# Two more value units on GpSimd, and a new order of the first two rows, in a graph-attention kernel

## The chip, the cores and the metric

The kernel runs on one core of one Trainium2 chip. The metric is the device time of one execution in microseconds (us), the median of a few executions. TensorE is called PE below, VectorE DVE, ScalarE ACT, GpSimd POOL and SyncE SP, as in the profile.

## What is computed

The reference normalises x (8192 x 256), takes the ReLU of it, averages the result over the neighbours in a dense 8192 x 8192 integer adjacency matrix with attention weights, and adds x. The attention's two score vectors f1 and f2 come from a second input through one small linear layer.

```python
h = jnp.maximum(_layernorm(x, axis=-1), 0.0)
# inside the layer: inlayer = h
hid = inlayer2 @ W.T + b
f1, f2 = hid @ w1 + b1, hid @ w2 + b2
logits = f1[:, None] + f2[None, :]
coefs = softmax(leaky_relu(logits, 0.01) + where(adj > 0, 0, -1e9), axis=-1)
return x + coefs @ inlayer
```

## The kernel before, in words

**Steady state.** The output's 8192 rows are taken 128 at a time, as 64 row tiles `I`. For one row tile the 8192 neighbours are two chunks `c` of 4096, and the weights of a chunk are made in four parts `g` (a group of 32 rows each) and turned in four strips, so that a row tile has eight parts and eight strips `k` of 1024 neighbours. The steps for one row tile are:

- SP loads the adjacency of a chunk into `adj_sb` (512 KB per transfer, four of them a chunk, one for each quadrant of partitions; `load_adj`, L335).
- ACT turns a part into a mask (`mask_part`, L540, recorded at L554). From row tile 1 on the mask lies in `mask` in SBUF; for row tile 0 it lies in PSUM rooms that are free then (`rp`, `acc`; `row0_mask`, L132).
- DVE makes the weights of a part (`weights`, L817, recorded at L824) from the packed words `b_word` and `c_word` and the mask, and turns each strip (`turn`, L828, recorded at L834) into one of four slots of `wT`.
- PE multiplies a strip with the values `H` (`products`, L1013): 8 blocks of 128 neighbours, three matmuls of 257 columns for each, two at L1024 (high and low part of the value, times the high part of the weight) and one at L1026. That is 24 matmuls a strip.
- DVE, ACT and POOL finish the row tile (`finish_0` to `finish_2`, `scale_rows`, `finish`), and SP stores it.

**Before the steady state** two things are made that all row tiles need. The first is the score part: the second input is loaded, turned on DVE (L718) and multiplied on PE (L979), and from f2 come the exponentials `D_big`, `D_inv` and b on ACT (L615, L616, L537), c (L622), and the packed words on DVE (`pack`, L807, recorded at L809 and L810). The second is the values: x is loaded in eight strips of 1024 rows (`load_x`, 256 KB a transfer, the quadrants 0 and 1 from SP's queue and 2 and 3 from ACT's queue, L333). The row statistics come from ACT for strips 0 and 1 (`sums`, `squares`, L584) and from DVE for the others (`raw_stats`, L765, and `variance`, L773). POOL makes 1/sqrt of the variance (`rstds`, a power, L411) and from it a factor and an offset for each row (`affine`, L423 to L433).

A **value unit** `n` is 512 rows (four blocks of 128 rows), 16 in all, two for each strip. `values(n)` applies the factor and the offset: four instructions of 256 columns, on ACT with a ReLU (L570) or, for the units in `values_on_pool`, on POOL without it (L460). `high_of_values(n)` writes the 16-bit high part, always on ACT (L576), with a ReLU. `low_of_values(n)` writes the low part: even units on POOL (L467), odd ones on DVE (L804), which takes the maximum with 0 first. Unit n uses float32 room n % 4, so it waits until the high and low part of unit n - 4 are there (`wait_slot`, L312). `D_column(k)` on POOL (L451) adds the column that gives the denominators. `sum_of_values(k)` on PE (L1038) sums the values of a strip with 16 + 16 small matmuls.

**Order.** Each engine works through its own list in the written order, and waits on semaphores of the others. For row tiles 0 and 1 the lists are written out by hand and interleaved with the making of the values: POOL's at L482 to L519, ACT's at L600 to L675, DVE's at L776 to L797 and L856 to L920, PE's at L1042 to L1072. PE's order is strips 0 to 3 of row tile 0 (with the sums of values 0 to 3), strips 0, 1, 2 of row tile 1, strip 4 of row tile 0, strip 3 of row tile 1, strip 5 of row tile 0, the sums 4 and 5, strips 4 and 5 of row tile 1, strip 6 of row tile 0, sum 6, strip 7 of row tile 0, strip 6 of row tile 1, sum 7, strip 7 of row tile 1. Then it waits for `h_sum` (DVE, L918) and makes the mean of the values (L1071), and row tile 2 begins. Strip 0 of row tile 0 (`products(0, 0, 0)`) needs turn (0, 0), the high and low parts of units 0 and 1, and `D_column(0)`; a later strip k of row tile 0 needs the same of units 2k and 2k + 1. Strips of row tile 1 need only their turn.

`two_rows` (L277) is the order in which the masks and the weights of row tiles 0 and 1 are made; the semaphore counts come from it. `first_adj` and `second_adj` (L354, L358) are the places where ACT's queue issues its half of the adjacency of row tiles 0 and 1; SP issues the other half.

Of the kernel before, what the change touches and what calls it, by code (L numbers as in the profile page):

```python
# [45 lines left out]
def graph_attention(nc, x, adj, inlayer2, W, b, w1, b1, w2, b2, out):  # L46
# [26 lines left out]
    with ExitStack() as ctx:  # L73
# [200 lines left out]
        def is_row(I, n):  # L274
            return type(I) is int and I == n

        two_rows = ((0, 0, 0), (0, 1, 0), (0, 2, 0), (0, 3, 0), (0, 0, 1), (0, 1, 1), (1, 0, 0),  # L277
                    (1, 1, 0), (1, 2, 0), (1, 3, 0), (0, 2, 1), (0, 3, 1), (1, 0, 1), (1, 1, 1),
# [23 lines left out]
        values_on_pool = (3, 7, 11, 15)  # L302
# [90 lines left out]
        def _(pool):  # L393
# [89 lines left out]
            rstds(2)  # L483
            scale_D()
            affine(0)
            rstds(1)
            rstds(3)
            affine(1)
            parts_of_D()
            low_of_values(0)  # L490
            values(3)
            affine(2)
            D_column(0)
            affine(3)
            low_of_values(2)
            rstds(4)
            D_column(1)
            low_of_values(4)
            values(7)
            D_column(2)  # L500
            D_column(3)
            affine(4)
            low_of_values(6)
# [6 lines left out]
            D_column(4)  # L510
            low_of_values(10)
            rstds(7)
            D_column(5)
            affine(7)
            values(15)
            D_column(6)
            low_of_values(12)
            D_column(7)
            low_of_values(14)  # L519
# [4 lines left out]
        def _(act):  # L524
# [94 lines left out]
            b_of_chunk(1)  # L619
            values(0)  # L620
# [22 lines left out]
            high_of_values(6)  # L643
            high_of_values(7)
            mask_part(0, 1, 1)
# [4 lines left out]
            mask_part(0, 2, 1)  # L650
# [41 lines left out]
        def _(dve):  # L692
# [88 lines left out]
            raw_stats(20, 24)  # L781
# [4 lines left out]
            variance(2)  # L786
            raw_stats(24, 28)
# [73 lines left out]
            weights(0, 0, 0)  # L861
            raw_stats(36, 40)
            raw_stats(40, 44)
            weights(0, 1, 0)
            weights(0, 2, 0)
            variance(4)
            raw_stats(44, 48)
            weights(0, 3, 0)
            raw_stats(48, 52)
            turn(0, 0)  # L870
            low_of_values(1)
            low_of_values(3)
            turn(0, 1)
            raw_stats(56, 60)
            raw_stats(52, 56)
            variance(5)
            turn(0, 2)
            variance(6)
            turn(0, 3)
            low_of_values(5)  # L880
            low_of_values(7)
            weights(0, 0, 1)
            weights(0, 1, 1)
# [5 lines left out]
            weights(0, 2, 1)  # L889
# [3 lines left out]
            raw_stats(60, 64)  # L893
            low_of_values(9)
            turn(0, 4)
            variance(7)
            turn(1, 3)
            low_of_values(11)
            weights(1, 0, 1)
            turn(0, 5)  # L900
# [10 lines left out]
            weights(2, 0, 0)  # L911
            weights(2, 1, 0)
# [5 lines left out]
            nc.vector.tensor_scalar(h_sum[:, :], hs_ps, 1.0 / (H_SCALE * N), None, ALU.mult).then_inc(h_sum_ready, 1)  # L918
            weights(2, 2, 0)
# [41 lines left out]
        def _(pe):  # L961
# [142 lines left out]
```

## Time and profile before

| | |
|---|---|
| median of 3 runs | 1448.58 us (1448.45 to 1448.86) |
| the profiled execution's own time | 1447.21 us |
| its span | 1445.4 us |
| PE busy | 1408.1 us (97%) |
| DVE busy | 1279.7 us (89%) |
| ACT busy | 612.4 us (42%) |
| POOL busy | 267.6 us (19%) |
| chain that ended last: PE acc L1024 and L1026 | 61% and 30% of the span |
| HBM | 209 GB/s over the span |

The span is the time from the first to the last instruction of the program. The profile takes PE as busy while a matmul is in flight, and matmuls overlap: the mean L1024 matmul is recorded at 273 ns, but one starts every 110 ns. A group's "idle before" is the time in which the engine did nothing just before its instructions, with the releaser that ended most of it.

### The profile page before, as it was taken

What the parts mean: (1) busy time and instruction counts of PE and PEld (TensorE: products, weight loads), DVE (VectorE), ACT (ScalarE), POOL (GpSimd) and SP (SyncE); (2) the same over time, 40 slices, a digit from 0 to 9 for tenths busy, and PEclk for the clock granted to TensorE, in tenths of its full rate; (3) what the DMA queues carried; (4) which work ended last, traced back from release to release, by engine and by line L of the source; (5) the groups of instructions that cost most, each with busy time, mean ns of one, the idle gap of its engine ahead of it and who ended that gap; (6) DMA issues with size and microseconds to landing.
All of it is one profiled execution on the core that took longest, in us unless ns stands there. A gap on an engine that the chain in (4) does not pass through costs nothing.

```text
span 1445.4 us, 33386 instructions
## 1 busy us (share of the span) xinstructions
PE 1408.1 (97%) x12623; PEld 1246.3 (86%) x12623; DVE 1279.7 (89%) x1313; ACT 612.4 (42%) x714; POOL 267.6 (19%) x269
## 2 busy tenths in 40 slices
PE   8489999999999999999999999999999999999998
PEld 7377888888888888888888888888888888888887
DVE  5899999989899898989989898998989989898994
ACT  2895344344444343444434344343434434344430
POOL 0582111101111110111111011111101111110111
PEclk9789999999999999999999999999999999999999
DMA  9978999999999999999999999999999999999940
GB/s 301 310 181 181 234 230 230 231 232 220 208 211 215 209 211 209 215 209 210 215 209 210 207 216 211 209 215 209 210 207 217 209 211 215 207 212 207 215 103 8
DMA packets 110168, 302.43 MB, mean 209 GB/s; under 512 B 11716, under 2 KB 44612, under 8 KB 110148
## 3 DMA queue, kind: packets, MB, share of 16 engines
q1 hardware_dynamic: 100144, 289.58, 89.4%
q10 hardware_dynamic: 10004, 12.59, 2.9%
q8 instruction: 12, 0.20, 0.1%
q14 instruction: 8, 0.07, 0.0%
HBM read 293.73 MB, written 8.39 MB: 209 GB/s over the span
## 4 chain that ended last, share of the span: by engine, by line
PE 94%; ACT 2%; DVE 2%; DMA 1%; issue 1%; ACTq 0%; POOL 0%; SPq 0%; POOLq 0%; DVEq 0%
PE acc L1024 61%; PE acc L1026 30%; PE rp L979 2%; DMA adj_sb<-in_adj_dram 1%; DVE wgt L824 1%; ACT h_f L570 1%; DVE wT L834 0%; ACT H L576 0%; PE rp L993 0%; ACT o_room L584 0%; DMA w<-in_L_gnn_w_dram 0%; PE small L966 0%; ACT rp L554 0%; DVE b_word L810 0%; ACT mask L554 0%
## 5 line engine op out<-in xcount | busy, mean ns | idle before, releaser
L1024 PE MATMUL acc<-H,wT 128*128 128x257 f16 x8192 | 1356.2, 273 | 9.7 <-DVE wT L834 6.9
L1026 PE MATMUL acc<-H,wT 128*128 128x257 f16 x4096 | 1120.0, 273 | 0.0
L1024 PEld LDWEIGHTS acc<-H,wT 128*128 128x128 bf16 x8192 | 802.1, 98 | 113.0 <-DVE wT L834 6.9
L554 ACT ACTIVATE mask<-adj_sb 128x1024 bf16<-128x1024 int32 x504 | 519.2, 1053 | 542.8 <-DVE wgt L824 428.8
L834 DVE STREAM_TRANSPOSE wT<-wgt 128x1024 f32<-128x1024 f32 x512 | 634.0, 1239 | 129.2 <-PE acc L1026 129.1
L824 DVE SCALAR_TENSOR_TENSOR wgt<-b_word,c_word,mask 128x1024 f32<-128x1024 f32 x504 | 626.9, 1256 | 0.0
L1026 PEld LDWEIGHTS acc<-H,wT 128*128 128x128 f16 x4096 | 401.5, 98 | 50.5
L474 POOL TENSOR_TENSOR x_res<-o_room,x_res 128x256 f32<-128x256 f32 x64 | 66.5, 1039 | 1115.2 <-ACT o_room L561 1069.5
L561 ACT ACTIVATE o_room<-acc,r_den 128x256 f32<-128x256 f32 x64 | 30.2, 471 | 251.0 <-DVE r_den L853 251.0
L479 POOL TENSOR_TENSOR o_room<-o_room,x_res 128x256 f32<-128x256 f32 x64 | 82.3, 1287 | 5.3
L476 POOL TENSOR_SCALAR o_room<-h_mean,no_nb 128x256 f32<-128x256 f32 x64 | 60.8, 950 | 0.0
L979 PE MATMUL rp<-wT,h_f 128*128 128x256 f32 x128 | 28.0, 381 | 0.0
L979 PEld LDWEIGHTS rp<-wT,h_f 128*128 128x128 f32 x128 | 24.5, 192 | 3.3
L570 ACT ACTIVATE h_f<-H,h_add,h_mul 128x256 f32<-128x256 f32 x48 | 24.7, 588 | 1.0 <-issue 1.0
L467 POOL TENSOR_TENSOR H<-h_f,H 128x1024 f16<-128x1024 f32 x8 | 17.8, 2226 | 4.0 <-ACT H L576 4.0
L411 POOL TENSOR_TENSOR rstd<-var_eps,minus_half 128x8 f32<-128x8 f32 x8 | 14.7, 1845 | 13.8 <-DVE var_eps L773 13.7
L1045 PE MATMUL small<-ones 128*128 128x128 f32 x20 | 4.6, 429 | 11.8 <-DVE wgt L824 11.8
L765 DVE BATCH_NORM_STATS2 stats<-H 128x6 f32<-128x512 f32 x24 | 15.3, 688 | 0.8 <-DMA H<-in_x_dram 0.8
L843 DVE TENSOR_SCALAR no_nb<-acc 128x1 f32<-128x1 f32 x64 | 7.7, 120 | 9.2 <-PE acc L1026 9.2
L1045 PEld LDWEIGHTS small<-ones 128*128 128x128 f32 x20 | 4.3, 331 | 12.0 <-DVE wgt L824 12.0
L718 DVE STREAM_TRANSPOSE wT<-wgt 128x1024 f32<-128x1024 f32 x8 | 9.5, 1222 | 5.7 <-DMA wgt<-in_L_gnn_inlayer_dram 3.6
L718 DVE STREAM_TRANSPOSE wT<-adj_sb 128x1024 f32<-128x1024 f32 x8 | 9.5, 1225 | 4.3 <-PE rp L979 4.3
(91 smaller groups left out, 173.2 us busy)
## 6 DMA issues: line engine op xcount, KB each, us to landing
adj_sb<-in_adj_dram SPq DMA_DIRECT2D x504, 512.0 KB, 8.6
x_res<-in_x_dram SPq DMA_DIRECT2D x64, 128.0 KB, 4.0
out_dram<-o_room SPq DMA_DIRECT2D x64, 128.0 KB, 4.2
H<-in_x_dram ACTq DMA_DIRECT2D x16, 256.0 KB, 12.2
H<-in_x_dram SPq DMA_DIRECT2D x16, 256.0 KB, 12.7
adj_sb<-in_adj_dram ACTq DMA_DIRECT2D x8, 512.0 KB, 13.1
wgt<-in_L_gnn_inlayer_dram ACTq DMA_DIRECT2D x8, 256.0 KB, 9.0
wgt<-in_L_gnn_inlayer_dram SPq DMA_DIRECT2D x8, 256.0 KB, 9.6
```

What stands on the lines that cost most here:

```text
L474: nc.gpsimd.tensor_tensor(x_res[:, par, :], o_raw[:, par, :], x_res[:, par, :], ALU.add).then_inc(pool_step, 1)
L476: nc.gpsimd.tensor_scalar(o_sb[:, par, :], h_mean[:, :], no_nb[:, par:par + 1], None, ALU.mult).then_inc(pool_step, 1)
L479: nc.gpsimd.tensor_tensor(o_sb[:, par, :], o_sb[:, par, :], x_res[:, par, :], ALU.add).then_inc(o_ready, 1)
L554: nc.scalar.activation(place, adj_sb[:, c, g * CQ:(g + 1) * CQ], ACT.Relu, scale=M_SCALE).then_inc(m_ready, 1)
L561: nc.scalar.activation(o_raw[:, par, :], acc[:, par, 0:D], ACT.Copy, scale=r_den[:, par:par + 1]).then_inc(scaled, 1)
L570: nc.scalar.activation(h_slot(n)[:, t, :], x_stage(n // 2)[:, j % TS, :], ACT.Relu, scale=h_mul[:, j:j + 1], bias=h_add[:, j:j + 1]).then_ ...
L718: nc.vector.transpose(in2T[:, k % 2, :, :].rearrange("p m (t s) -> p t m s", t=TS)[:, HALF * e:HALF * (e + 1), :, :], in2_stage(k)[:, HALF ...
L824: nc.vector.scalar_tensor_tensor(out=wgt[:, wgt_slot(I, c), g, :], in0=b_word[:, c * CQ:(c + 1) * CQ], scalar=c_word[:, bass.ds(Q * I + g, ...
L834: nc.vector.transpose(wT[:, wT_slot(I, k), :, :].rearrange("p t (g r) -> p g t r", g=Q), wgt[:, wgt_slot(I, c), :, s * SQ:(s + 1) * SQ]).t ...
L979: mm = pe.matmul(rp[:, k // SC, SQ * (k % SC):SQ * (k % SC + 1)], V[:, m, :], in2T[:, k % 2, m, :], start=(m == 0), stop=(m == FM - 1))
L1024: pe.matmul(acc[:, par, 0:DV], w_hi[:, slot, t, :], H[:, j, part, 0:DV], start=(j == 0 and part == 0), stop=False)
L1026: mm = pe.matmul(acc[:, par, 0:DV], w_lo[:, slot, t, :], H[:, j, 0, 0:DV], start=False, stop=(j == ROWS - 1))
```

## The change

`values_on_pool` gets the units 5 and 13 beside 3, 7, 11 and 15, so POOL makes the affine part of six units and ACT of ten. On ACT's list x strips 4 and 5 are issued after `squares(1)`, strip 6 after the exponentials of b, strip 7 after `high_of_values(0)`, and `f_to_sbuf(0)` comes after `squares(0)`. In `two_rows` part (0, 2, 1) comes before row tile 1's first parts. POOL, ACT and DVE get new orders for the first two row tiles: on DVE `low_of_values(1)` comes before turn (0, 0), two pairs of statistics come after it, part (0, 2, 1) comes before row tile 1's, and parts (2, 0, 0) and (2, 1, 0) come after `h_sum`. On PE `sum_of_values(4)` comes one place earlier. Nothing is changed from row tile 2's strips on, and no computation is added or left out.

```diff
-        two_rows = ((0, 0, 0), ..., (0, 0, 1), (0, 1, 1), (1, 0, 0),
-                    (1, 1, 0), (1, 2, 0), (1, 3, 0), (0, 2, 1), (0, 3, 1), ...
+        two_rows = ((0, 0, 0), ..., (0, 0, 1), (0, 1, 1), (0, 2, 1),
+                    (1, 0, 0), (1, 1, 0), (1, 2, 0), (1, 3, 0), (0, 3, 1), ...
-        values_on_pool = (3, 7, 11, 15)
+        values_on_pool = (3, 5, 7, 11, 13, 15)
-            rstd_order = (0, 2, 1, 3, 4, 5, 6, 7)
+            rstd_order = (0, 1, 3, 2, 4, 5, 6, 7)
```

POOL's list after the change, in full:

```python
rstds(0); rstds(1); scale_D(); affine(0); parts_of_D(); rstds(3); rstds(2); affine(1); affine(2)
values(3); D_column(0); D_column(1); low_of_values(0); affine(3); values(5); low_of_values(2)
D_column(2); low_of_values(4); values(7); low_of_values(6); rstds(4); D_column(3); affine(4)
rstds(5); rstds(6); affine(5); affine(6); values(11); low_of_values(8); D_column(4); values(13)
D_column(5); low_of_values(10); rstds(7); affine(7); low_of_values(12); D_column(6); values(15)
low_of_values(14); D_column(7)
```

ACT's list (the core of the diff):

```diff
             sums(0)
             load_x(act, 1, 2, (2, 3))
-            f_to_sbuf(0)
             load_x(act, 2, 3, (2, 3))
             squares(0)
             load_x(act, 3, 4, (2, 3))
+            f_to_sbuf(0)
             first_adj(act, 0, (2, 3))
-            load_x(act, 4, 5, (2, 3))
             sums(1)
             f_to_sbuf(1)
+            squares(1)
+            load_x(act, 4, 5, (2, 3))
             load_x(act, 5, 6, (2, 3))
-            squares(1)
-            load_x(act, 6, 7, (2, 3))
-            load_x(act, 7, 8, (2, 3))
...
             b_of_chunk(0)
             b_of_chunk(1)
+            load_x(act, 6, 7, (2, 3))
+            mask_part(0, 0, 0)
             values(0)
...
+            values(1)
             high_of_values(0)
-            mask_part(0, 0, 0)
+            load_x(act, 7, 8, (2, 3))
             mask_part(0, 1, 0)
             first_adj(act, 1, (2, 3))
             mask_part(0, 2, 0)
-            mask_part(0, 3, 0)
-            values(1)
             high_of_values(1)
             values(2)
+            mask_part(0, 3, 0)
             high_of_values(2)
+            values(4)
             second_adj(act, 0, (2, 3))
-            values(4)
             high_of_values(3)
             high_of_values(4)
-            values(5)
             high_of_values(5)
```

DVE's list from the packed words to the end of the two row tiles (w is `weights`, t `turn`, lo `low_of_values`, st `raw_stats` by its first block):

```text
before: pack; st32; w(0,0,0); st36; st40; w(0,1,0); w(0,2,0); var4; st44; w(0,3,0); st48; t(0,0); lo1; lo3; t(0,1);
        st56; st52; var5; t(0,2); var6; t(0,3); lo5; lo7; w(0,0,1); w(0,1,1); w(1,0..3,0); t(1,0); w(0,2,1);
        t(1,1); w(0,3,1); t(1,2); st60; lo9; t(0,4); var7; t(1,3); lo11; w(1,0,1); t(0,5); w(1,1..3,1); t(1,4);
        t(1,5); t(0,6); lo13; t(0,7); t(1,6); lo15; w(2,0,0); w(2,1,0); t(1,7); finish 0; h_sum; w(2,2,0); w(2,3,0)
after:  pack; st32; w(0,0,0); st40; st36; st44; w(0,1,0); lo1; w(0,2,0); w(0,3,0); var4; t(0,0); var5; t(0,1);
        lo3; t(0,2); st48; t(0,3); st52; w(0,0,1); w(0,1,1); var6; lo5; lo7; w(0,2,1); w(1,0..3,0); t(1,0); st56;
        t(1,1); w(0,3,1); t(1,2); lo9; t(0,4); st60; t(1,3); var7; t(0,5); lo11; w(1,0..3,1); t(1,4);
        t(1,5); t(0,6); lo13; t(0,7); t(1,6); lo15; t(1,7); finish 0; h_sum; w(2,0,0); w(2,1,0); w(2,2,0); w(2,3,0)
```

## Rows read from the trace of the kernel before

**Rows 1.** The page's part 5: PE's costliest group and the waits before it.

```profile
L1024 PE MATMUL acc<-H,wT 128*128 128x257 f16 x8192 | 1356.2, 273 | 9.7 <-DVE wT L834 6.9
```

**Rows 2.** Busy time by stretch: length, then PE, PEld, DVE, ACT, POOL, PEclk, DMA share, GB/s.

```profile
90.60:93.50 2.90, 2.86 (x14) 2.02 (x15) 2.90 (x3) 2.90 (x7) 2.90 (x4) 0.51 1.02 275
...
140.00:1440.00 1300.00, 1299.55 (x11815) 1155.69 (x11812) 1161.54 (x1164) 523.41 (x546) 202.86 (x186) 1.00 0.93 206
```

**Rows 3.** Timeline of PE: start us, length us, engine, line, operation, count [idle before, releaser].

```profile
70.95 0.59 PE L1024 MATMUL acc<-H,wT 128*128 128x257 f16 x2 [2.74 <-DVE H L804]
...
90.64 0.61 PE L1024 MATMUL acc<-H,wT 128*128 128x257 f16 x2 [4.28 <-DVE wT L834]
...
110.06 0.40 PE L1024 MATMUL acc<-H,wT 128*128 128x257 f16 x2 [0.57 <-DVE wT L834]
...
124.25 0.61 PE L1038 MATMUL small<-H,D_inv_parts 128*2 128x256 f16 x16
...
129.15 0.38 PE L1024 MATMUL acc<-H,wT 128*128 128x257 f16 x2 [1.11 <-DVE wT L834]
...
132.58 0.39 PE L1024 MATMUL acc<-H,wT 128*128 128x257 f16 x2 [0.63 <-DVE wT L834]
```

**Rows 4.** Timeline of ACT and its queue (ACTq), 46 to 58 us.

```profile
46.46 2.85 ACTq L333 DMA_DIRECT2D H<-in_x_dram  x1
...
49.34 1.42 ACTq L333 DMA_DIRECT2D H<-in_x_dram  x1
50.80 0.26 ACT L615 ACTIVATE D_big<-f_rel 128x64 f32<-128x64 f32 x1 [3.27 <-issue]
...
51.11 2.10 ACT L537 ACTIVATE wgt<-rp,tiny 128x1024 f32<-128x1024 f32 x2
53.10 2.08 ACT L570 ACTIVATE h_f<-H,h_add,h_mul 128x256 f32<-128x256 f32 x4
...
55.34 1.06 ACT L576 ACTIVATE H<-h_f 128x1024 f16<-128x1024 f32 x1
...
56.28 1.97 ACT L554 ACTIVATE rp<-adj_sb 128x1024 f32<-128x1024 int32 x2
```

**Rows 5.** Timeline of DVE, from f2_rel to row tile 2.

```profile
48.48 0.25 DVE L790 TENSOR_SCALAR f_rel<-f_col,tiny 128x64 f32<-128x64 f32 x1
...
50.50 0.17 DVE L773 TENSOR_SCALAR var_eps<-stats 128x8 f32<-128x8 f32 x1
52.24 0.76 DVE L809 TENSOR_SCALAR b_word<-wgt 128x1024 bf16<-128x1024 bf16 x1 [1.58 <-ACT wgt L537]
...
57.42 1.30 DVE L765 BATCH_NORM_STATS2 stats<-H 128x6 f32<-128x512 f32 x2
...
77.88 1.18 DVE L804 SCALAR_TENSOR_TENSOR H<-h_f,H 128x1024 f16<-128x1024 f32 x1
79.09 3.05 DVE L804 SCALAR_TENSOR_TENSOR H<-o_room,H 128x1024 f16<-128x1024 f32 x1
...
96.33 2.87 DVE L804 SCALAR_TENSOR_TENSOR H<-h_f,H 128x1024 f16<-128x1024 f32 x1
...
124.91 0.42 DVE L918 TENSOR_SCALAR h_sum<-small 128x256 f32<-128x256 f32 x1 [2.30 <-PE small L1038]
125.25 2.47 DVE L824 SCALAR_TENSOR_TENSOR wgt<-b_word,c_word,mask 128x1024 f32<-128x1024 f32 x2
```

**Rows 6.** Timeline of POOL, 60 to 115 us.

```profile
61.89 2.17 POOL L460 TENSOR_SCALAR o_room<-H,h_mul,h_add 128x256 f32<-128x256 f32 x4
...
78.18 2.88 POOL L467 TENSOR_TENSOR H<-h_f,H 128x1024 f16<-128x1024 f32 x1 [0.37 <-ACT H L576]
81.02 4.23 POOL L411 TENSOR_TENSOR rstd<-var_eps,minus_half 128x8 f32<-128x8 f32 x2
...
104.46 5.22 POOL L460 TENSOR_SCALAR o_room<-H,h_mul,h_add 128x256 f32<-128x256 f32 x4
...
112.02 2.13 POOL L467 TENSOR_TENSOR H<-h_f,H 128x1024 f16<-128x1024 f32 x1
```

More of the change, by code:

```diff
@@ L482, in _ @@
             rstds(0)
-            rstds(2)
+            rstds(1)
             scale_D()
             affine(0)
-            rstds(1)
+            parts_of_D()
             rstds(3)
+            rstds(2)
             affine(1)
-            parts_of_D()
+            affine(2)
+            values(3)
+            D_column(0)
+            D_column(1)
             low_of_values(0)
-            values(3)
-            affine(2)
-            D_column(0)
             affine(3)
+            values(5)
             low_of_values(2)
-            rstds(4)
-            D_column(1)
+            D_column(2)
             low_of_values(4)
             values(7)
-            D_column(2)
+            low_of_values(6)
+            rstds(4)
             D_column(3)
             affine(4)
-            low_of_values(6)
             rstds(5)
@@ L510, in _ @@
             D_column(4)
+            values(13)
+            D_column(5)
             low_of_values(10)
             rstds(7)
-            D_column(5)
             affine(7)
+            low_of_values(12)
+            D_column(6)
             values(15)
-            D_column(6)
-            low_of_values(12)
+            low_of_values(14)
             D_column(7)
-            low_of_values(14)
             pool.wait_ge(h_mean_done, 1)
@@ L643, in _ @@
             high_of_values(6)
+            mask_part(0, 1, 1)
+            mask_part(0, 2, 1)
             high_of_values(7)
-            mask_part(0, 1, 1)
             mask_part(1, 0, 0)
@@ L780, in _ @@
             chunk_f(1)
-            raw_stats(20, 24)
+            raw_stats(24, 28)
             dve.wait_ge(u_ready, Q + 1)
@@ L785, in _ @@
             nc.vector.reduce_max(tiny[0:1, 1:2], fm_ps, AX.X).then_inc(f_max_ready, 1)
-            variance(2)
-            raw_stats(24, 28)
+            raw_stats(20, 24)
             dve.wait_ge(F_ps_ready, 1)
@@ L792, in _ @@
             nc.vector.tensor_scalar(tiny[:, 3:4], F_ps, SLOPE - 1.0, None, ALU.mult).then_inc(f_offset_ready, 1)
+            variance(2)
             raw_stats(28, 32)
+            variance(3)
             then_wait(nc.vector.tensor_tensor(tiny[:, 5:6], tiny[:, 4:5], tiny[:, 2:3], ALU.add))
@@ L861, in _ @@
             weights(0, 0, 0)
+            raw_stats(40, 44)
             raw_stats(36, 40)
-            raw_stats(40, 44)
+            raw_stats(44, 48)
             weights(0, 1, 0)
+            low_of_values(1)
             weights(0, 2, 0)
+            weights(0, 3, 0)
             variance(4)
-            raw_stats(44, 48)
-            weights(0, 3, 0)
-            raw_stats(48, 52)
[L870 to L874, printed above, removed]
+            turn(0, 0)
+            variance(5)
+            turn(0, 1)
+            low_of_values(3)
+            turn(0, 2)
+            raw_stats(48, 52)
+            turn(0, 3)
             raw_stats(52, 56)
-            variance(5)
-            turn(0, 2)
+            weights(0, 0, 1)
+            weights(0, 1, 1)
             variance(6)
-            turn(0, 3)
             low_of_values(5)
             low_of_values(7)
-            weights(0, 0, 1)
-            weights(0, 1, 1)
+            weights(0, 2, 1)
             weights(1, 0, 0)
@@ L888, in _ @@
             turn(1, 0)
-            weights(0, 2, 1)
+            raw_stats(56, 60)
             turn(1, 1)
@@ L892, in _ @@
             turn(1, 2)
-            raw_stats(60, 64)
             low_of_values(9)
             turn(0, 4)
+            raw_stats(60, 64)
+            turn(1, 3)
             variance(7)
-            turn(1, 3)
+            turn(0, 5)
             low_of_values(11)
             weights(1, 0, 1)
-            turn(0, 5)
             weights(1, 1, 1)
@@ L918, in _ @@
             nc.vector.tensor_scalar(h_sum[:, :], hs_ps, 1.0 / (H_SCALE * N), None, ALU.mult).then_inc(h_sum_ready, 1)
+            weights(2, 0, 0)
+            weights(2, 1, 0)
             weights(2, 2, 0)
```

25 lines of the change are left out of this document (10 added, 15 removed).

## The prediction

> **What bounds the kernel now.** I read the page's groups first, then the busy time by stretch, then the timelines of the first 140 us. PE is the bound of nearly everything: from 140 to 1440 us it starts 11,815 matmuls in 1300 us, one every 0.110 us, at full clock and without idle time [rows 2]. All PE's waits for turned strips are 6.9 us [rows 1], and they lie before 133 us. From the last wait of 0.63 us at 132.58 [rows 3] on, the rest of the kernel is fixed: it ends 1445.4 - 132.6 = 1312.8 us later. The change leaves it alone, so its worth is how far that point (strip 1 of row tile 2, "the anchor") moves. A shift of 2.9 us is 0.2% of the time, which is about what a measurement of this kernel can tell from no change.
>
> Before the anchor PE waits at 70.95 (2.74 us), 90.64 (4.28), 110.06 (0.57), 129.15 (1.11) and 132.58 (0.63), each time but the first for a turn, and the first for a low part, all from DVE [rows 3]. DVE, in turn, has one idle time of note before it packs b: 1.58 us, waiting for ACT's exponential [rows 5]. From 52.24 to the turn that the strip at 110.06 waited for it works without a gap. So up to strip 4 of row tile 1 (PE at 110.06) **DVE is the bound**; from there to 124.25 + 0.6 = 124.85, the end of the last sum of values, PE is, with 14.8 us of its own work; then DVE again: `h_sum`, two weights, a turn, two weights, a turn, 7.7 us up to the anchor.
>
> **The change, part by part.** I sum along DVE's list.
>
> *The x issues behind the exponentials.* ACT's queue issued strip 7's two transfers for 2.85 and 1.42 us, and D_big waited 3.27 us for nothing else ("issue"); it began at 50.80 [rows 4]. In the new order strips 4 and 5 are issued there, not 6 and 7, so the queue holds four transfers fewer than when strip 7's had to wait, and I expect short issues. DVE has f2_rel at 48.48 + 0.25 [rows 5], so D_big starts at 48.9; the two small exponentials and the first b (0.3 + 1.05 us) are done at 50.3. DVE is free only at 50.50 + 0.17 [rows 5], with the same small steps to do in the new order. It packs at 50.75 instead of 52.24: **1.5 us gained**. Bounds: 0 if the issues block as before, 1.6 if DVE is free a little sooner. The transfers issued later are covered: ACT's queue still has its adjacency transfers in flight at 46 us, keeps its order, and strip 4's data are wanted by DVE only after the packing, at 56 us. SP's list and its issues are unchanged. In the worst case DVE's statistics wait as long as the issue is late, a microsecond or two, and that is in the range.
>
> *DVE's work up to turn (1, 4).* Both lists hold the same instructions between the packing and this turn (16 of L765, 16 weights, 6 low parts, the turns), so reordering them costs nothing by itself. What differs is what they run into. A low part on DVE takes 1.18 us (at 77.88) [rows 5]. The one at 79.09 took 3.05, with POOL's low part (78.18 to 81.06) beside it [rows 6], and the one at 96.33 took 2.87: 1.87 + 1.69 = **3.56 us lost in collisions** before. The Trainium skill ("SBUF — State Buffer", Who interferes with whom) calls the pair's shared port an exclusive lock, held for a whole instruction, and says elsewhere on that page that a DVE instruction with two SBUF inputs takes part in it. By that rule the two low parts are such a pair, and the trace agrees.
>
> New collisions, from the new lists. (a) ACT, from 48.9: exponentials 2.3 us to 51.2, mask 0.98, values 2.0, c 0.3, values 2.0, high 0.94, two masks, high, values(2) 2.08 [rows 4]: 62.3. POOL's `D_column(1)` waits for that, then low(0) runs 62.3 to 64.4. DVE's new early low(1) comes at 50.75 + 5.2 (packing, 52.24 to 57.42) + 8 x 0.61 + 2 x 1.19 = 63.2 and waits **1.2 us**. (b) DVE's low(3) comes at 70.5, after two weights and two turns; POOL's low(2) has just ended (64.4, affine(3) and a wait 1.6, values(5) 2.17, low 2.13: 70.3) and low(4) is next: 0 or 2.1 us, I take **1.0**. (c) low(11) at 99 us against POOL's low(10), begun at 97.4: **0.5**. low(5), low(7) and low(9) find POOL at powers or small steps. Sum 2.7 instead of 3.56, with ends at 0.3 and 6. So turn (1, 4) and PE's strip behind it move by -1.5 - 3.56 + 2.7 = **-2.4 us**.
>
> *PE's wait at 90.64.* Strip 0 of row tile 0 starts when turn (0, 0) ends: low(1) done at 65.5, two weights 2.4, variance 0.1, turn 1.2, so 69.3 instead of 70.95. The strip at 90.64 moves by -1.5 - 1.87 + 2.2 = -1.2, to 89.5, and the idle time before it is 2 to 4 us instead of 4.28. After 4.28 us idle the clock was at 0.51 in the next 2.9 us [rows 2], which costs about 1.45 us of matmuls. Whether or not it falls now, it is hidden: up to the strip at 110.06 PE has six strips (6 x 24 x 0.110) and two sums (1.1), 17 us, and DVE's path takes 19.4 - 1.69 + 0.5 = 18.2.
>
> *Two units more on POOL.* ACT saves 2 x 2.08 us [rows 4]; after 52.24 DVE waits for ACT nowhere up to this turn, so this is worth nothing by itself. POOL gets 2 x 2.17 us (at 61.89) [rows 6]. values(5) runs beside weights whose mask is in PSUM and values(13) beside statistics and turns, none of them seen to collide. Before, column 7 and low(14) were done at 114.15 [rows 6] and PE took strip 7 of row tile 0 two strips before the sum at 124.25 [rows 3], at 118.9. I put low(14) and column 7 at 115.1 (114.15, plus values(13) 2.17, less the earlier start) and PE's arrival at 116.5: hidden with 1.4 us in hand. Nothing, and up to 4.7 us if that cover goes.
>
> *The weights moved behind `h_sum`.* Before, DVE had (2, 0, 0) and (2, 1, 0) made while it waited 2.30 us for the last sum [rows 5]. Now all four come after `h_sum`, on the path to turn (2, 0). Two weights are 2.47 us there: **2.4 us lost**, in full, since PE has only a strip and the mean, 3.2 us, for a DVE path of 129.15 - 124.85 + 2.4 = 6.7. PE then idles 3.5 us instead of 1.11. If the clock falls as it did after 4.28 us, strip 0 of row tile 2 takes 1.45 us longer, of which about 0.7 is left behind DVE's next turn. Ends 1.2 and 3.8.
>
> Sum for the anchor: -2.4 + 2.4 = **0.0**, with the clock's 0.7 against a few tenths in the stretch from 110 to 124.85 that a tighter order may close. In the profiled execution: span 1445.4, own time 1447.21, 1.8 us around it; the median of the runs, 1448.58, stands 1.4 us above it. I forecast **no change, 1448.4 us**, its own range 1446.5 to 1450.6.
>
> **The rivals.**
>
> *Faster: no collision at all.* Then DVE gains 1.5 + 3.56, less a few tenths, 4.9; minus 2.4 is -2.5 us, and with 0.6 closed between 110 and 124.85 -3.1: 1445.5 us. For it: orders like these decide a collision by tenths. Against it: (a) follows from sums with little play. 0.14.
>
> *Slower: POOL's chain at strip 7 of row tile 0.* values(15) took 5.22 us instead of 2.17 beside DVE's run of weights (1, 1..3, 1) (at 104.46) [rows 6]: 3.05 us. In the new list `rstds(7)` and affine(7) fall into that run, with low(12), column 6, values(15), low(14) and column 7 queued behind them. It decides from 1.4 us of delay. One such delay gives +1.6 (inside the forecast's range), two +4.7: 1453.1 us. For it: that row. Against: DVE's run is short, and after it come turns. 0.12.
>
> *Slower: GpSimd's added work locks DVE out.* Eight added instructions of 0.55 us that all hold up DVE's critical list: +4.4, 1452.8 us. The trace speaks against part of it: the first power at 81.02 ran 1.64 us while DVE finished its low part from 81.06 to 82.14. [...] 0.06.
>
> *The start doesn't move:* strips 4 and 5 block ACT's queue as strip 7 did. Then +1.5: 1449.9 us. 0.08.
>
> **How the numbers follow.** The forecast has 0.60 (0.56 within 0.2%, 0.01 faster, 0.03 slower), the faster rival 0.14, the two slower ones 0.18, the last 0.08, within. That is faster 0.15, same 0.64, slower 0.21. The range reaches from just inside the faster rival, 1445.5, to 1452.0, short of the slower ones.
>
> **What would show it.** Right: D_big near 48.9 with no 2.85 us issue before it; a DVE L804 of over 2 us near 63; PE's first strip near 69.3; the strip of turn (1, 4) near 107.7; an idle time of about 3.5 us before row tile 2; the anchor at 132.6. Wrong: a PE wait before strip 7 of row tile 0 (rival POOL), an anchor before 130 or after 135, or any new PE wait after it.

## The result and the profile after

The changed kernel takes 1452.78 us (median of 10 runs, 1450.74 to 1455.53) against 1448.84 (10 runs, 1448.45 to 1449.56): ratio 1.0028, 95% interval 1.0020 to 1.0035. It is 3.9 us slower, and outside the range. The profiled execution took 1453.29 us with a span of 1451.5; it lies 0.5 us above its median, where the one of before lies 1.6 below the 1448.84. So the two traces differ by 6.1 us, and the medians by 3.9: some 2 us of what follows belong to these two executions and not to the kernels.

The page's part 5 of the changed kernel has TensorE's group of [rows 1], with 2.9 us more of idle time:

```profile
L1024 PE MATMUL acc<-H,wT 128*128 128x257 f16 x8192 | 1358.4, 274 | 12.6 <-DVE wT L834 7.7
```

TensorE's timeline of the changed kernel, the strips that stand in [rows 3] and two more:

```profile
71.26 0.61 PE L1024 MATMUL acc<-H,wT 128*128 128x257 f16 x2 [2.08 <-DVE wT L834]
...
83.96 0.38 PE L1024 MATMUL acc<-H,wT 128*128 128x257 f16 x2 [4.50 <-POOL H L451]
...
111.46 0.57 PE L1024 MATMUL acc<-H,wT 128*128 128x257 f16 x2 [2.11 <-DVE wT L834]
...
115.78 0.38 PE L1024 MATMUL acc<-H,wT 128*128 128x257 f16 x2
...
127.08 0.61 PE L1038 MATMUL small<-H,D_inv_parts 128*2 128x256 f16 x16
...
134.37 0.38 PE L1024 MATMUL acc<-H,wT 128*128 128x257 f16 x2 [3.50 <-DVE wT L834]
...
138.49 0.57 PE L1024 MATMUL acc<-H,wT 128*128 128x257 f16 x2
```

Busy time by stretch, same kernel, columns as in [rows 2]:

```profile
111.50:114.40 2.90, 2.90 (x14) 2.02 (x15) 2.90 (x3) 2.90 (x5) 2.90 (x5) 0.51 1.04 225
...
134.30:137.20 2.90, 2.83 (x19) 2.21 (x20) 2.90 (x3) 0.44 (x1) 0.00 (x0) 0.70 1.03 223
...
140.00:1440.00 1300.00, 1300.00 (x11821) 1156.52 (x11819) 1166.23 (x1170) 526.22 (x546) 205.61 (x189) 1.00 0.93 206
```

Read these against before, point by point. Strip 4 of row tile 1 is at 111.46 for 110.06: **+1.4**. The last sum is at 127.08 for 124.25, +2.8: **1.4 more**. There the strip begun at 111.46 lasted 4.32 us to the next one's start (115.78), at a granted clock of 0.51, which is the 1.2 GHz level; at full clock a strip takes 24 x 0.110 = 2.65. Of these 1.7 us, 0.2 were made up by 127.08. The first strip of row tile 2 is at 134.37 for 129.15, +5.2: **2.4 more**, the idle time of 3.50 for 1.11. The anchor is at 138.49 for 132.58, +5.9: **0.7 more**, again at a lowered clock. The 4.50 us of waiting at 83.96, before strip 2 of row tile 0, stand where before had none; the clock was at 0.55 behind them. The row names POOL's column of 83.28, but the third column, which strip 2 needs, was made at 72.08; what it needed last is DVE's low(5), which ended at 83.71. The wait has slack: TensorE was waiting again at 111.46. Behind the anchor next to nothing differs: 1451.5 - 138.5 = 1313.0 us for 1312.8, and the stretch from 140 to 1440 is as full as before.

What DVE did, the rows that answer to [rows 5]:

```profile
49.20 0.25 DVE L789 TENSOR_SCALAR f_rel<-f_col,tiny 128x64 f32<-128x64 f32 x1
...
51.54 0.78 DVE L809 TENSOR_SCALAR b_word<-wgt 128x1024 bf16<-128x1024 bf16 x1
...
56.34 0.31 DVE L809 TENSOR_SCALAR c_word<-c_f 128x256 bf16<-128x256 bf16 x1 [0.45 <-ACT c_f L624]
...
64.41 2.97 DVE L804 SCALAR_TENSOR_TENSOR H<-h_f,H 128x1024 f16<-128x1024 f32 x1
...
71.13 3.25 DVE L773 TENSOR_SCALAR var_eps<-stats 128x8 f32<-128x8 f32 x1
72.13 2.26 DVE L834 STREAM_TRANSPOSE wT<-wgt 128x1024 f32<-128x1024 f32 x1
73.29 2.15 DVE L804 SCALAR_TENSOR_TENSOR H<-o_room,H 128x1024 f16<-128x1024 f32 x1
...
82.50 1.21 DVE L804 SCALAR_TENSOR_TENSOR H<-h_f,H 128x1024 f16<-128x1024 f32 x1
...
103.02 2.32 DVE L804 SCALAR_TENSOR_TENSOR H<-o_room,H 128x1024 f16<-128x1024 f32 x1 [0.47 <-ACT H L578]
...
127.74 0.42 DVE L916 TENSOR_SCALAR h_sum<-small 128x256 f32<-128x256 f32 x1 [2.65 <-PE small L1038]
128.08 4.86 DVE L824 SCALAR_TENSOR_TENSOR wgt<-b_word,c_word,mask 128x1024 f32<-128x1024 f32 x4
132.98 1.25 DVE L834 STREAM_TRANSPOSE wT<-wgt 128x1024 f32<-128x1024 f32 x1
```

And what POOL and ACT did at those times:

```profile
64.18 2.13 POOL L467 TENSOR_TENSOR H<-h_f,H 128x1024 f16<-128x1024 f32 x1
...
67.87 2.18 POOL L460 TENSOR_SCALAR h_f<-H,h_mul,h_add 128x256 f32<-128x256 f32 x4
70.00 2.13 POOL L467 TENSOR_TENSOR H<-h_f,H 128x1024 f16<-128x1024 f32 x1
...
72.23 2.13 POOL L467 TENSOR_TENSOR H<-h_f,H 128x1024 f16<-128x1024 f32 x1
...
81.69 1.63 POOL L411 TENSOR_TENSOR rstd<-var_eps,minus_half 128x8 f32<-128x8 f32 x1
...
102.12 2.15 POOL L467 TENSOR_TENSOR H<-h_f,H 128x1024 f16<-128x1024 f32 x1 [1.67 <-ACT H L578]
...
112.40 3.25 POOL L460 TENSOR_SCALAR o_room<-H,h_mul,h_add 128x256 f32<-128x256 f32 x4
...
117.70 1.27 POOL L451 COPY H<-D_parts 128x16 f16<-128x16 f16 x1
```

```profile
49.48 0.26 ACT L615 ACTIVATE D_big<-f_rel 128x64 f32<-128x64 f32 x1 [1.36 <-DVE f_rel L789]
...
75.34 1.03 ACT L556 ACTIVATE rp<-adj_sb 128x1024 f32<-128x1024 int32 x1 [4.01 <-DMA adj_sb<-in_adj_dram]
```

Against 1.18 us, DVE's low(1) at 64.41 lost 1.79 us, low(3) at 73.29 0.97, low(11) at 103.02 1.14. The variance at 71.13, 0.05 us of work, let the next turn start only at 72.13, the moment POOL's low part of 70.00 ended: 0.95 (its recorded 3.25 us runs on under its successors; how late the next one starts is what counts). Each of the four overlaps a POOL L467, and each is over when that one ends and its own 1.2 us or less have passed. That is 4.9 us, and with two waits for ACT (0.45 and 0.47) 5.8 us, where before lost 3.56 in collisions. ACT's mask at 75.34 waited 4.01 us for the second adjacency chunk of row tile 0 ("the chunk" below); before, no such wait was there. DVE did not wait for this mask: from 57 to 102 us it has no idle time in this trace.

### The profile page after: what moved, and what is told of

Same layout as the page of the kernel before. It is cut to its first block, busy times and chain, and to the rows that moved or that the text cites. A ratio compares the mean times of both kernels' runs of the same rounds, so it can differ in the third digit from the quotient of the medians.

```text
span 1451.5 us, 33386 instructions
## 1 busy us (share of the span) xinstructions
PE 1410.7 (97%) x12623; PEld 1247.9 (86%) x12623; DVE 1279.7 (88%) x1313; ACT 610.7 (42%) x706; POOL 272.1 (19%) x277
## 4 chain that ended last, share of the span: by engine, by line
PE 93%; DVE 3%; DMA 2%; ACT 1%; issue 1%; POOL 0%; SPq 0%; POOLq 0%; ACTq 0%; DVEq 0%
PE acc L1024 61%; PE acc L1026 30%; DMA adj_sb<-in_adj_dram 2%; PE rp L979 1%; DVE wgt L824 1%; DVE stats L765 0%; DVE wT L834 0%; PE rp L993 0%; DVE H L804 0%; ACT mask L556 0%; DMA w<-in_L_gnn_w_dram 0%; PE small L966 0%; DVE var_eps L773 0%; ACT H L578 0%; ACT rp L556 0%
## 5 line engine op out<-in xcount | busy, mean ns | idle before, releaser
L572 ACT ACTIVATE h_f<-H,h_add,h_mul 128x256 f32<-128x256 f32 x40 | 20.6, 587 | 4.1 <-POOL h_add L433 2.6
L467 POOL TENSOR_TENSOR H<-h_f,H 128x1024 f16<-128x1024 f32 x8 | 17.1, 2132 | 3.5 <-ACT H L578 3.5
```

Source lines behind the costliest of these rows:

```text
L572: nc.scalar.activation(h_slot(n)[:, t, :], x_stage(n // 2)[:, j % TS, :], ACT.Relu, scale=h_mul[:, j:j + 1], bias=h_add[:, j:j + 1]).then_ ...
```

## The experiments

Each is timed beside the kernel before. "Undone" is an edit of the changed kernel, "alone" one of the kernel before. Differences between kernels are differences of medians, each against the 1452.78 or some 1448.9 us; taken from the ratios they come out up to 0.5 us otherwise. Against the changed kernel (ratio 1.0020 to 1.0035) of its edits only `a_w2early`, `a_rows` and `a_comb` stand clear; the intervals of `a_xbefore`, `a_x45`, `a_pool4`, `a_nocol` and `a_warm` overlap it, so that their differences, 0.8 to 2.2 us, are indications.

**The tail undone** (`a_w2early`).

```
             low_of_values(15)
+            weights(2, 0, 0)
+            weights(2, 1, 0)
             turn(1, 7)
...
-            weights(2, 0, 0)
-            weights(2, 1, 0)
             weights(2, 2, 0)
```

> The changed kernel, with weights (2, 0, 0) and (2, 1, 0) back before turn (1, 7). Tail theory: PE's wait before row tile 2 falls from 3.5 to about 1.1 us and the clock stays up behind it, so 3.1 us less than the changed kernel (2.4 of DVE's work and 0.7 of the slow clock): ratio to the kernel before about 1.0007. Rival (the tail is worth little since DVE's later turns or POOL's chain set the pace): less than 1 us, ratio 1.002 or more.

Measured: 1449.4 us (1448.18 to 1453.45), ratio 1.0004 (0.9995 to 1.0013), 3.4 us less than the changed kernel. TensorE's waits in the tail are those of before:

```profile
135.38 0.38 PE L1024 MATMUL acc<-H,wT 128*128 128x257 f16 x2 [1.11 <-DVE wT L834]
...
138.81 0.39 PE L1024 MATMUL acc<-H,wT 128*128 128x257 f16 x2 [0.63 <-DVE wT L834]
```

This profile is of the slowest of its 11 executions; the lengths of the two waits are what counts. Its lists up to the tail are those of the changed kernel, and yet strip 4 of row tile 1 starts at 114.87 there, for 111.46, after 4.09 us of waiting. So much do two executions of one order differ ahead of the tail.

**The tail alone** (`b_w2late`): the same move made in the kernel before.

> The kernel before, with weights (2, 0, 0) and (2, 1, 0) moved behind h_sum. Tail theory: +2.4 us, and +0.7 where the clock falls after 3.5 us of PE idle: ratio 1.0017 to 1.0022. Rival: below 1.0007.

Measured: 1452.25 us (1450.06 to 1453.68), ratio 1.0025 (1.0016 to 1.0034), **+3.3 us** against the 1448.91 beside it. Its trace has the 3.50 us, and the lowered clock behind it:

```profile
133.02 0.38 PE L1024 MATMUL acc<-H,wT 128*128 128x257 f16 x2 [3.50 <-DVE wT L834]
...
137.32 0.38 PE L1024 MATMUL acc<-H,wT 128*128 128x257 f16 x2
```

```profile
133.00:136.00 3.00, 2.98 (x17) 2.25 (x18) 3.00 (x3) 0.00 (x0) 0.00 (x0) 0.61 1.02 220
```

The move costs 3.4 us in the one direction and 3.3 in the other. By this trace 2.4 are the weights (3.50 for 1.11 us of waiting) and 0.9 the clock: the second strip starts 4.30 us after the first, for 3.43 before.

**The x issues undone** (`a_xbefore`): ACT issues strips 4 to 7 where it did before the change.

> The changed kernel with ACT's issues of x strips 4 to 7 where they were before. DMA theory (the late issues leave ACT's queue empty from about 49 to 51.5 us, chunk 1 of row tile 0 lands at 75.3 instead of 70.9, and PE waits 4.5 us before strip 3 of row tile 0): the chunk lands near 71 again, mask (0, 0, 1) doesn't wait, PE's wait before strip 3 is under 2 us, D_big starts near 50.8, and the time is 1 to 2 us below the changed kernel, ratio near 1.002. Rival (the wait before strip 3 is hidden behind DVE's list, and what counts is D_big's start): slower than the changed kernel by up to 1.3 us, ratio near 1.0035.

Measured: 1453.6 us (1452.33 to 1455.82), ratio 1.0039 (1.0025 to 1.0053), not faster. The chunk landed 3 us sooner, at 72.2, and no time was gained: ACT's mask of part (0, 2, 1) now waited 5.00 us for DVE's weights, where it had waited 0.97 in the changed kernel, with the high part of unit 7 behind it:

```profile
82.70 1.03 ACT L556 ACTIVATE rp<-adj_sb 128x1024 f32<-128x1024 int32 x1 [5.00 <-DVE wgt L824]
```

The edit moves two things against each other: the issues blocked again, D_big began at 52.01 and packing at 53.45, 1.9 us later than in the changed kernel. So it prices neither alone. That the late chunk cost the changed kernel little is seen in that kernel's own trace, in which DVE never waits for the mask.

**The x issues alone** (`b_xlate`): the kernel before with the changed kernel's x issues.

> The kernel before with x strips 4 and 5 issued behind the squares, 6 behind the exponentials, 7 behind the first high part. DMA theory: D_big starts 1.3 us earlier, but chunk 1 of row tile 0 lands 4 us later and mask (0, 0, 1), with ACT's list behind it, waits 1 to 2 us: ratio 1.000 to 1.0015. Rival (my forecast's step): 1.0 to 1.5 us gained, ratio 0.999.

Measured: 1447.84 us (1446.06 to 1451.51), ratio 0.9994 (0.9985 to 1.0003). D_big is at 49.12, 1.7 us earlier than the 50.80 of [rows 4], but ACT's mask then waits for the chunk that is queued behind the x strips, and DVE's low(7) behind that:

```profile
77.18 1.03 ACT L554 ACTIVATE rp<-adj_sb 128x1024 f32<-128x1024 int32 x1 [4.21 <-DMA adj_sb<-in_adj_dram]
```

```profile
82.35 2.30 DVE L804 SCALAR_TENSOR_TENSOR H<-o_room,H 128x1024 f16<-128x1024 f32 x1 [4.40 <-ACT H L576]
```

**Strips 6 and 7 alone late** (`b_x67`): strips 4 and 5 stay, so ACT's queue does not run empty between 49 and 51 us, where it moved 0.01 MB in the changed kernel and 0.32 before; here it moves 0.25.

```
-            load_x(act, 6, 7, (2, 3))
-            load_x(act, 7, 8, (2, 3))
             act.wait_ge(f2_rel_ready, 1)
...
             b_of_chunk(1)
+            load_x(act, 6, 7, (2, 3))
             values(0)
...
             high_of_values(0)
+            load_x(act, 7, 8, (2, 3))
```

> The kernel before with only x strips 6 and 7 issued later by ACT (6 behind the exponentials of b, 7 behind the first high part), 4 and 5 as before. Start theory: D_big starts right behind f2_rel, 1.3 us earlier, ACT's DMA queue doesn't run empty, chunk 1 of row tile 0 lands near 71 us; 1.0 to 1.5 us less than before, ratio 0.9990 to 0.9993. Rival (PE's waits absorb it, or a collision moves): 1.000.

Measured: **1446.16 us** (1444.97 to 1446.56), ratio 0.9980 (0.9971 to 0.9989): faster than both kernels. D_big is as early as in the changed kernel and the wait for the chunk is nearly gone:

```profile
49.29 0.26 ACT L613 ACTIVATE D_big<-f_rel 128x64 f32<-128x64 f32 x1 [1.23 <-DVE f_rel L790]
```

```profile
73.12 1.03 ACT L554 ACTIVATE rp<-adj_sb 128x1024 f32<-128x1024 int32 x1 [0.23 <-DMA adj_sb<-in_adj_dram]
```

**Strips 4 and 5 undone** (`a_x45`): the same idea in the changed kernel.

> Changed kernel with ScalarE's issues of x strips 4 and 5 where they stood before (strip 4's behind strip 3's, ahead of the squares), strips 6 and 7 late as in the change. Theory that the emptied queue of ScalarE (49 to 51.5 us) gives away what the shorter issues bring: b_x67 against b_xlate was 1.7 us faster, so the changed kernel comes to about 1451 us, ratio 1.0016, and row tile 0's second chunk lands near 73 us, not 75.3 us. Rival, that behind it the late turn (0,1) and the wait for GpSimd's values hold strip 2 anyway: no difference, 1.0028, with TensorE's wait before 84 us still 4 us or more.

Measured: 1451.26 us (1449.75 to 1452.66), ratio 1.0014 (1.0005 to 1.0023). The time came as the theory had it, 1.5 us less, but not by its mechanism: the chunk was no earlier (mask at 75.07, 3.49 us of waiting) and strip 2 waited as long (4.49 us before 84.18). ACT's queue was not empty (0.26 MB between 49 and 51 us), so the emptied queue isn't what makes the chunk late in the changed kernel. In the kernel before, leaving strips 4 and 5 in place brought it 4 us sooner (`b_x67` against `b_xlate`); here only strips 6 and 7 back in place did (`a_xbefore`). Why is open. What differs in the trace is that after a wait of 1.57 us before strip 4 of row tile 1 the clock did not fall.

**Two units back on ACT** (`a_pool4`) and **two units on POOL alone** (`b_pool6`): units 5 and 13.

> The changed kernel with value units 5 and 13 back on ACT (after the high parts of 4 and of nothing else: values(5) before high_of_values(5), values(13) before high_of_values(13)), all other orders as changed. POOL theory (the two units load the queue on which low parts collide with DVE's): some collisions go, 0.5 to 2 us less than the changed kernel, ratio 1.0015 to 1.0025. Order theory (the units are hidden, the order of low parts and of part (0, 2, 1) is what costs): within 0.5 us of the changed kernel, ratio near 1.003. If ACT's 4 us matter, slower: 1.004.

> The kernel before with value units 5 and 13 on POOL, in its own order (5 behind low part 4, 13 behind column 5). POOL theory: 4.3 us more on POOL delay low part 6, column 3 and strip 7's chain, ratio 1.0005 to 1.003. Order theory (hidden): ratio 0.9995 to 1.0005.

Measured: undone 1451.52 us (1450.01 to 1453.85), ratio 1.0022 (1.0013 to 1.0032), 1.3 less than the changed kernel; alone 1450.67 (1449.73 to 1451.45), ratio 1.0012 (1.0003 to 1.0021), 1.8 more than before. So the two units cost 1.8 us alone and are not free; the 1.3 agrees, within overlapping intervals. In `a_pool4` DVE's low(3) took 1.18 us, no longer 2.15: without values(5), POOL's low(2) was over at 69.99 and its low(4) began only at 73.50. But DVE then waited 2.69 us for the mask behind the late chunk, and the strip of turn (1, 4) came no earlier (111.51); what differs there is that its clock stayed up, after 1.33 us of waiting. In `b_pool6` POOL's values(5) begins only at 74.87, behind POOL's low(4), and ACT stands:

```profile
77.06 1.06 ACT L578 ACTIVATE H<-h_f 128x1024 f16<-128x1024 f32 x1 [5.13 <-POOL h_f L460]
```

**Collisions taken out** (`a_nocol`): DVE's low(1) behind two more weights, variance(5) later.

```
             weights(0, 1, 0)
-            low_of_values(1)
...
             variance(4)
+            low_of_values(1)
             turn(0, 0)
-            variance(5)
             turn(0, 1)
...
             raw_stats(52, 56)
+            variance(5)
```

> The changed kernel with two of DVE's steps moved out of the way of POOL's low parts: low part 1 behind weights (0, 2, 0) and (0, 3, 0), variance(5) behind the statistics of blocks 52 to 55. Collision theory (low part 1 took 2.97 us instead of 1.18, and a variance and turn lost 0.95 beside POOL's low part 2): DVE reaches turn (1, 0) about 2.5 us earlier, the wait for turn (1, 4) goes from 2.11 to under 0.7 us, and the time is 2 to 3.5 us less, ratio 1.0005 to 1.0015. Rival (the collisions only move elsewhere, or PE's own work from strip 3 of row tile 0 on sets the pace): under 1 us, ratio 1.002 or more.

Measured: 1450.73 us (1449.15 to 1454.51), ratio 1.0017 (1.0008 to 1.0026), 2.0 less than the changed kernel. Both low parts are undisturbed, and the strip of turn (1, 4) comes 2.1 us earlier:

```profile
66.60 1.21 DVE L804 SCALAR_TENSOR_TENSOR H<-h_f,H 128x1024 f16<-128x1024 f32 x1
...
70.03 1.24 DVE L804 SCALAR_TENSOR_TENSOR H<-o_room,H 128x1024 f16<-128x1024 f32 x1
```

```profile
109.38 0.39 PE L1024 MATMUL acc<-H,wT 128*128 128x257 f16 x2 [1.99 <-DVE wT L834]
```

```profile
109.40:112.30 2.90, 2.90 (x27) 2.58 (x28) 2.90 (x3) 2.90 (x5) 2.90 (x5) 1.00 1.04 226
```

After 1.99 us the clock stayed at 1.00, where after 2.11 it went to 0.51.

**The order of row tiles 0 and 1 undone** (`a_rows`): weights and mask of part (0, 2, 1) behind row tile 1's first parts, as before.

> Changed kernel with the order of the parts of row tiles 0 and 1 as before the change: the weights (0,2,1) and its mask behind row tile 1's first four parts. Theory that the reordering costs time (ScalarE's mask (0,2,1) waits for weights in front of the exponentials of strip 7 and row tile 1's masks, VectorE's first turn of row tile 1 begins 1.5 us later than before): 1 to 1.5 us less than the changed kernel, ratio about 1.002, and turn (1,0) back at about 89.5 us. Rival, that the order only exchanges which turn waits: within 0.5 us of the changed kernel, and the wait goes to strip 6 or 7 of row tile 0.

Measured: 1456.37 us (1455.7 to 1457.61), ratio 1.0050 (1.0037 to 1.0064): **3.6 us more** than the changed kernel. Theory and rival both fall. With six units on POOL the new order is a help: without it the wait before strip 2 of row tile 0 is 6.22 us, the one before the strip of turn (1, 4) 3.40, and the low clock follows both (0.50).

```profile
86.19 0.59 PE L1024 MATMUL acc<-H,wT 128*128 128x257 f16 x2 [6.22 <-POOL H L451]
...
115.88 0.61 PE L1024 MATMUL acc<-H,wT 128*128 128x257 f16 x2 [3.40 <-DVE wT L834]
```

A part of this may be the chunk, which landed later (ACT's wait 5.58 us for 4.01) though the edit does not touch it: DVE waits 1.63 us for the mask behind it, where the changed kernel's DVE does not. The landing varies between 73 and 78 us over the kernels whose x strips are issued late. Why it varies stays open.

**TensorE kept busy in the tail** (`a_warm`): 13 matmuls of ones, whose result nobody reads, behind the mean's.

```
+            for n in range(13):
+                pe.matmul(small[:, 1, 0:P], ones[:, :], ones[:, :], start=True, stop=True)
```

> Changed kernel with 13 matmuls of ones (128 x 128) behind the mean's matmul, in the 3.50 us in which TensorE idled before row tile 2's first strip; their result is not read. Theory that the low granted clock behind that wait is part of the change's price: the clock stays at 0.99 or more in the first strips of row tile 2, their spacing goes from 4.1 us back to 3.4 us, 0.7 to 1.3 us less than the changed kernel, ratio to before about 1.002. Rival, that the clock costs nothing there, because the second strip waits for VectorE's turn anyway: no difference from the changed kernel (1.0028). If the matmuls reach past the turn's end they cost up to 1 us instead.

Measured: 1450.55 us (1450.23 to 1451.4), ratio 1.0012 (1.0003 to 1.0021), 2.2 less than the changed kernel and more than expected. The clock of the tail is at 1.00, and its second strip starts 3.43 us after the first, not 4.12:

```profile
132.37 0.38 PE L1024 MATMUL acc<-H,wT 128*128 128x257 f16 x2 [0.60 <-DVE wT L834]
...
135.80 0.39 PE L1024 MATMUL acc<-H,wT 128*128 128x257 f16 x2 [0.63 <-DVE wT L834]
```

```profile
132.30:135.20 2.90, 2.80 (x24) 2.28 (x24) 2.90 (x3) 2.12 (x3) 0.00 (x0) 1.00 1.04 225
```

That is 0.7 us. The rest of this profile's lead lies ahead of the edit: strip 4 of row tile 1 waited 1.75 us and its clock did not fall. Whether the added matmuls are the cause of the rest in the medians, too, is not settled.

**Three parts undone at once** (`a_comb`): `a_w2early`, `a_nocol` and `a_x45` together.

> Changed kernel with three parts undone at once: the two weights of row tile 2 ahead of turn (1,7) again, low(1) and variance(5) moved off GpSimd's low parts, x strips 4 and 5 issued as before. Alone these gave 3.4, 2.0 and 1.5 us. Theory that the change's price is the tail plus collisions and waits on the way to the turns, two stages with nothing between them that absorbs a delay: at least the tail and one of the other two add, median 1447.4 us or less (ratio 0.999 or less); if all three add, 1445.9 us (0.998). Rival, that a third bound common to the three sets the start of row tile 2 (the high parts on ScalarE or GpSimd's chain), which a_w2early has already reached: 1449.4 us, ratio 1.0004, and the wait before strip 4 or 5 of row tile 1 grows by what the front gains.

Measured: 1447.13 us (1446.29 to 1450.54), ratio 0.9991 (0.9982 to 1.0000), 5.7 less than the changed kernel, of 6.9 if all added in full. They do add nearly, and no common bound holds them. The interval ends at 1.0000, so this kernel is level with the one before or a little faster, with the six units and the new order still in it. Strip 4 of row tile 1 is at 110.29 (1.79 us of waiting) at a clock of 1.00, the anchor at 132.57:

```profile
110.30:113.20 2.90, 2.90 (x27) 2.58 (x28) 2.90 (x3) 2.90 (x5) 2.90 (x5) 1.00 1.04 225
129.10:132.00 2.90, 2.80 (x24) 2.28 (x24) 2.90 (x3) 2.30 (x3) 0.00 (x0) 1.00 1.03 230
```

**The best of before** (`b_best`): `b_x67`, with DVE's low(7) behind the weights (0, 0, 1) and (0, 1, 1) and low(9) ahead of `raw_stats(60, 64)`.

> Kernel before with x strips 6 and 7 issued later by ScalarE (as in b_x67), and on top VectorE's low(7) behind the weights (0,0,1) and (0,1,1), and low(9) ahead of raw_stats(60,64). Theory that collisions of VectorE's two-operand low parts with GpSimd's values are time on the way to the turns: in b_x67 low(7) took 2.82 us and low(9) 3.08 us against 1.2 us undisturbed, so 1.6 + 1.9 us are to be had; the strip 1 of row tile 2 comes up to 3 us earlier than in b_x67, median about 1443 us, ratio to before about 0.996. Rival, that the collisions only move to the next instruction on VectorE (the same GpSimd work is still there): ratio as b_x67, about 0.998, and the sum of the long durations on VectorE stays.

Measured: **1445.49 us** (1444.38 to 1447.29), ratio 0.9977 (0.9968 to 0.9986), 3.5 us better than before and the fastest here, though its interval overlaps that of `b_x67`. In `b_x67` low(9) was disturbed:

```profile
95.30 3.08 DVE L804 SCALAR_TENSOR_TENSOR H<-h_f,H 128x1024 f16<-128x1024 f32 x1
```

In `b_best` it takes 1.23, but stands behind a wait:

```profile
95.23 1.23 DVE L804 SCALAR_TENSOR_TENSOR H<-h_f,H 128x1024 f16<-128x1024 f32 x1 [2.94 <-ACT H L576]
```

The collisions went, as the theory said; the time did not, as the rival said, for a reason that neither had. Put earlier, low(9) finds ACT's high part not ready, and what was lost beside POOL is now lost waiting for ACT.

## Why the prediction was wrong

The frame held. DVE and TensorE before 133 us decide, the anchor carries the result (+5.9 of the traces' 6.1), and nothing behind it moved. The sum up to the anchor, 0.0, was wrong in two places. (It belongs to 1448.6 us; the forecast's 1448.4 has no term for the other 0.2.)

*The tail, +2.4 with "about 0.7" of clock: right in kind, a little short.* The trace shows +2.4 and +0.7 to the letter, and I left the 0.7 out of the sum against "a few tenths" that a tighter order might close; 0.2 closed, and the clock's 1.7 us at strip 4 of row tile 1 took more than that. Measured by itself the tail is 3.3 to 3.4 us. Error 1.0 us.

*The front, -2.4: this is the step that failed.* It came out +1.4 at the strip of turn (1, 4) in the trace, and +0.5 in the medians once the tail is taken off (1449.4 less 1448.9). By the traces DVE packed 0.7 us earlier and then took 2.1 us longer to turn (1, 4), where I had 1.5 us earlier and 0.9 shorter. Its terms:

- *The x issues, 1.5 us gained.* Packing began at 51.54, not 50.75: 0.7 gained. D_big did lose its "issue" wait, but f_rel came at 49.20 for 48.48 (it lies between 48.2 and 49.4 over the kernels here), and D_big waited for that. The start of before that I set out from was also an early one: in the other three kernels with the x issues of before, D_big began at 51.8 to 52.4 and packing at 53.2 to 53.8, for 50.80 and 52.24. What I called "covered" wasn't: with the late issues the chunk landed about 4 us later (75.3 for 70.9), and masks waited for it. Whether DVE then waits differs from run to run: not in the changed kernel's trace, 4.40 us in `b_xlate`, 2.69 in `a_pool4`, 1.63 in `a_rows`. Alone, the step is worth 1.1 us (0.9994, not surely different from nothing), and 2.7 us when only strips 6 and 7 are moved.
- *Collisions, "2.7 instead of 3.56".* They were 4.9, and 5.8 with the waits for ACT. (a) low(1) was expected at 63.2 and 1.2; it was at 64.41 and 1.79. (b) low(3) at 0.97 was right, but the variance before it, which I had as 0.1 us of harmless work, was held by POOL's low(2) and cost 0.95. (c) low(11) was 1.14 and 0.47 for 0.5. low(5), low(7) and low(9) were clean as said. 0.8 at the start and 3.1 here make the 3.8 us by which the strip missed, to a tenth. `a_nocol` takes out two of the collisions and gains 2.0 us.
- *Two units more on POOL, nothing.* They cost 1.3 us by the one run and 1.8 by the other. I costed them by whether strip 7 would be late. There was no wait, but by luck: column 7 was done at 118.97, not at 115.1, and TensorE needed it at 121.7, not at 116.5. Had TensorE kept to my sum and POOL not, the strip would have waited 2.5 us. Their price was elsewhere: they push POOL's other low parts into DVE's, (b) above, and in `b_pool6` ACT waits 5.13 us for values(5).
- *"Reordering costs nothing by itself."* Putting the order of row tiles 0 and 1 back costs the changed kernel 3.6 us, of which 1.6 may be the chunk. The list with six units on POOL needs the new order.

*The clock, "hidden".* At the strip of 90.64 there was no wait now, and no fall; the long wait (4.50 us) stood before strip 2 of row tile 0, for DVE's low(5), which I had not foreseen, and the fall behind it had slack. My own sum did not quite hide a fall, by the way: 17 + 1.45 us for TensorE against 18.2 for DVE. But the wait before strip 4 of row tile 1 grew from 0.57 to 2.11 us, the clock fell, and from there to the last sum TensorE is the bound: of 4.32 - 2.65 = 1.7 us, 1.4 were left at the last sum. I gave this place no clock price because I expected no wait there. `a_x45`, `a_pool4`, `a_nocol` and `a_comb`, with waits of 1.57, 1.33, 1.99 and 1.79, show no fall in that strip. Nor does it come in every execution of these lists: up to the tail `a_warm` and `a_w2early` have the changed kernel's, and the clock stayed up in the one (after 1.75 us) and fell in the other (0.60 in the next 2.9 us, after 4.09).

*The rivals.* The one with no collisions is refuted by the four long rows. POOL's chain at strip 7 didn't come. "GpSimd's added work locks DVE out" gave 1452.8, the measured time, but by another sum: not eight instructions of 0.55 us on the critical list, but POOL's low parts, displaced, in front of DVE's, and 3.4 us of tail. The rule of the Trainium skill ("SBUF — State Buffer", Who interferes with whom), by which a DVE instruction with two SBUF inputs contends with a GpSimd instruction that reads SBUF, is borne out for POOL's two-input L467: three low parts of DVE were held beside it, and the variance, which has one input, too. For the power at 81.69, beside which DVE's low(5) at 82.50 took 1.21 us, it wasn't, as before.

The budget, alone or undone, in medians: tail 3.3 to 3.4, two units 1.3 to 1.8, x issues -1.1 alone (-0.8 undone); the sum of these is 3.5 to 4.4, against 3.9 measured. Two of the terms, the 1.3 and the x issues, are within the noise of their own runs, so that the agreement proves little. The order and the collisions lie inside these terms, since they depend on one another.

## What to carry to other kernels

Here work that filled a wait cost its full length once it was put behind the wait, and the clock's price came on top: look for idle time that the move creates on TensorE just where it is the bound. A transfer issued later can make the ones queued behind it late too; move only the issues that block. Before an order is judged by one trace, look at a second execution of it: here the same lists put one strip at 111.1, 111.5 and 114.9 us. When a collision between two engines is removed by reordering, ask first whether the inputs are ready at the new place.

## What was new of the hardware

- The granted clock fell to half after 2.11 us of idle time and didn't after 1.99 or 1.75 (same strip, three kernels). The length alone does not decide: at other strips it stayed at 1.00 after 2.16 us (`b_pool6`, 85.73) and 2.09 (`b_best`, 87.72). After 3.50 us it fell in all seven profiles that have this gap, and it cost 0.7 to 0.9 us in six of them (0.7 in the changed kernel) and 1.7 in the seventh (`a_nocol`, whose second strip there began 5.11 us after the first, for 3.43).
- With 13 matmuls of ones in that gap it stayed up, which was worth 0.7 us in the trace; no cost was seen.
- A DVE instruction as small as the variance (0.1 to 0.4 us otherwise) can be held for a microsecond beside a two-input POOL instruction.
- Two x issues on ACT's queue took 2.85 and 1.42 us before (4.06 and 1.44 in `a_xbefore`), and 0.3 to 0.5 each where they came behind the exponentials. That fewer transfers were then outstanding is the likely cause; no run varies it alone.
